# Token sums on VectorE, and the output products of experts 0 to 5 inside the routed loop's last six steps

## The reference

```
gate_logits = x @ gate_weight.T                 # 16 experts
top_vals, top_idx = top_k(gate_logits, 2)
routing_w = softmax(top_vals)
h = silu(einsum('td,efd->tef', x, w1))          # w1[e]: 256 x 512
h_sum = einsum('tef,te->ef', h, mask)           # sum over the tokens that chose e
h_mean = h_sum / maximum(counts, 1)[:, None]
y_mean = einsum('ef,edf->ed', h_mean, w2)       # w2[e]: 512 x 256
out = einsum('tk,tkd->td', routing_w, y_mean[top_idx])
```

## Time and profile before

| | us |
|---|---|
| median of 3 runs | 1165.25 |
| the profiled execution's own time | 1164.0 |
| its span in the trace | 1162.4 |
| start of the first tile's matmuls (L1925) | 1039.07 |
| end of the routed loop's matmuls, start of the last sums (L1912) | 1121.20 |
| first output product (L1856) | 1124.69 |
| transposes of `yT` (L1948) | 1148.06 |

### The profile page before, as it was taken

The page is one execution under the profiler, slowest core; times in us unless marked ns, Lnnn a source line. Parts: engine busy times, 40 slices in busy tenths (PEclk is TensorE's granted clock), DMA queues, the critical chain, the costliest instruction groups (busy, mean ns, idle before and its releaser), DMA issues. The chain is left out here.

```text
span 1162.4 us, 19075 instructions
## 1 busy us (share of the span) xinstructions
PE 1063.3 (91%) x5694; PEld 886.5 (76%) x5694; DVE 964.7 (83%) x1633; ACT 839.8 (72%) x1029; POOL 666.6 (57%) x522
## 2 busy tenths in 40 slices
PE   2993999999999999999999999999859998579985
PEld 2772788888888888888888888888647776579983
DVE  6751699999999999999999999999966887684357
ACT  3212799999999999999999999999724544434442
POOL 3245787877878777877788777874241221133410
PEclk9997999999999999999999999999979999779985
DMA  6736766666666666666666666665020311624455
GB/s 180 261 113 147 156 127 135 134 130 132 134 131 132 135 133 132 133 133 128 130 132 133 135 127 138 127 130 134 1 73 10 116 45 45 211 88 132 149 172 182
DMA packets 129067, 148.77 MB, mean 128 GB/s; under 512 B 72573, under 2 KB 81158, under 8 KB 128893
## 3 DMA queue, kind: packets, MB, share of 16 engines
q0 software_dynamic: 38576, 97.54, 39.1%
q1 hardware_dynamic: 89611, 48.75, 15.9%
q10 hardware_dynamic: 786, 1.30, 0.3%
HBM read 137.00 MB, written 15.66 MB: 131 GB/s over the span
## 5 line engine op out<-in xcount | busy, mean ns | idle before, releaser
L1002 PE MATMUL ps<-W2h,w1l_w3l 128*128 128x512 f32 x1264 | 425.8, 398 | 0.0
L797 POOL DMA_INDIRECT gath<-dst_table,idx_sl x158 | 263.6, 1668 | 53.1 <-issue 47.4
L1002 PEld LDWEIGHTS ps<-W2h,w1l_w3l 128*128 128x128 f32 x1264 | 227.1, 189 | 38.5
L1002 PE MATMUL ps<-W2l,w1l_w3l 128*128 128x512 f32 x632 | 247.8, 392 | 0.0
L810 POOL DMA_INDIRECT gath<-src_table,idx_sl x156 | 187.5, 1202 | 102.3 <-PE ps L997 50.7
L1002 PEld LDWEIGHTS ps<-W2l,w1l_w3l 128*128 128x128 f32 x632 | 118.7, 188 | 27.0
L819 POOL TENSOR_TENSOR msg_lo<-act,msg_hi 128x512 fp32r<-128x512 f32 x77 | 122.9, 1596 | 24.9 <-DVE msg_hi L938 24.9
L888 DVE TENSOR_TENSOR agg<-agg,ps 125x512 f32 x166 | 114.1, 687 | 14.5 <-PE ps L1048 7.6
L844 ACT ACTIVATE act<-ps 128x1024 f32<-128x1024 f32 x79 | 81.2, 1027 | 37.0 <-PE ps L1034 37.0
L900 DVE SCALAR_TENSOR_TENSOR act<-act,ps 128x1024 f32<-128x1024 f32 x79 | 96.0, 1215 | 2.1 <-ACT act L865 2.1
L929 DVE TENSOR_TENSOR w1l_w3l<-act,w1l_w3l 128x1024 fp32r<-128x1024 f32 x79 | 96.3, 1219 | 0.0
(11 more groups left out here) (359 smaller groups left out, 2367.4 us busy)
## 6 DMA issues: line engine op xcount, KB each, us to landing
ea_sl<-ea_scr SPq DMA_DIRECT2D x158, 64.0 KB
w_raw<-in_L_ffn_w_dram SPq DMA_DIRECT2D x13, 512.0 KB, 4.4
w_more<-in_L_ffn_w_dram SPq DMA_DIRECT2D x12, 512.0 KB, 8.7
ea_scr<-in_edge_attr_dram POOLq DMA_DIRECT2D x1, 5000.0 KB
w_late<-in_L_ffn_w_dram SPq DMA_DIRECT2D x7, 512.0 KB, 6.2
w_raw<-in_L_gnn_W_dram SPq DMA_DIRECT2D x3, 1024.0 KB, 8.1
gath<-src_table,idx_sl POOLq DMA_INDIRECT x158
gath<-dst_table,idx_sl POOLq DMA_INDIRECT x158, 5.2
```

What stands on the lines that cost most here:

```text
L797: pool.indirect_dma_start(out=gath[:, k, j, :], out_offset=None, in_=dst_table[:, :], in_offset=bass.IndirectOffsetOnAxis(ap=idx_sl[:, p % ...
L1002: return nc.tensor.matmul(ps_2[:, p % 2, j, :], part[:, p % 2, d, j * P:(j + 1) * P], weights[:, d, :], start=False, stop=last)
```

## The change

1. **Token sums.** The two matmuls per tile on TensorE and the addition of two columns on VectorE go. In their place VectorE runs one `scalar_tensor_tensor` per tile, `acc[expert] += hs * valid`, on 128 partitions x 256, one step behind. The sum over the 128 partitions is left to the mean's matmul: ones (128x128) times `acc[:, e, :]` gives the sum on all partitions. `spread_hm`, `hsum` and `hm` go, and with them ScalarE's part. The division by the counts moves to the end, as one operation on `yT`.
2. **`acc` lies where `w_raw` was** (16 KB per partition), so GpSimd zeroes it between its fourth and its fifth gather, and all of `w2` is now loaded over `w1T`. SP loads experts 0 to 9 once 24 tiles have been multiplied, and 10 to 15 once 27 have.
3. **Inside the loop.** TensorE's mean of expert e, for e = 0 to 5, stands at the end of step 29 + e, and VectorE's four products of it in step 30 + e. Means 0 to 5 use the two banks of `ps_s`; 6 to 15 use four banks, `ps_n` and `ps_s`.
4. Each product now waits for the last but one (its scratch `junk_y` has two slots of 256).

```diff
+INSIDE, INSIDE_AT = 6, 29
...
-        w2_more = nc.alloc_sbuf_tensor_at("w2_more", [P, E - WS, KC, FFN], F32, offset=T["w1T_at"])
+        w2_all = nc.alloc_sbuf_tensor_at("w2_all", [P, E, KC, FFN], F32, offset=T["w1T_at"])
...
+        acc = T["w_raw"][:].rearrange("p a (c f) -> p (a c) f", f=FFN)
...
+        def mean_bank(e):
+            if e < INSIDE:
+                return ps_s[:, e % 2, 0:FFN]
+            return (ps_n, ps_s)[(e - INSIDE) // 2 % 2][:, e % 2, 0:FFN]
+
+        def mean_before(e):
+            return e - 2 if e < INSIDE else max(e - 4, INSIDE - 1)
...
-            for e in range(WS):
-                sp.wait_ge(S["w1T_ps"], (E - EARLY) * FC)
-                sp.wait_ge(S["h_ps"], RT * (e + 1) // (WS + 1))
-                sp.dma_start(w2_raw[:, e], w2_rows[e]).then_inc(w2_in[e], 16)
-
-            sp.wait_ge(S["h_ps"], RT)
-            for e in range(WS, E):
-                sp.dma_start(w2_more[:, e - WS], w2_rows[e]).then_inc(w2_in[e], 16)
+            for first, end, t in ((0, 10, 24), (10, E, 27)):
+                sp.wait_ge(S["h_ps"], t)
+                for e in range(first, end):
+                    sp.dma_start(w2_all[:, e], w2_rows[e]).then_inc(w2_in[e], 16)
...
             for t in range(RT):
+                if t == XG:
+                    pool.wait_ge(S["w1T_ps"], WS * FC)
+                    nc.gpsimd.memset(T["w_raw"][:], 0.0).then_inc(S["acc_zeroed"], 1)
...
-            act.wait_ge(S["hm_ready"], 1)
-            for e in range(E):
-                need(act, S["mean_ps"], e - 1)
-                for f in range(FC):
-                    ins = nc.scalar.activation(spread_hm[:, e % 2, f, :], ident[:], ACT.Copy, scale=hm[:, f, e:e + 1])
-                ins.then_inc(S["spread"], 1)
...
+            def products(e):
+                dve.wait_ge(w2_in[e], 16)
+                dve.wait_ge(S["mean_ps"], e + 1)
+                for q in range(KC):
+                    need(dve, S["y_step"], e * KC + q - 1)
+                    nc.vector.tensor_tensor_reduce(out=junk_y[:, q % 2, :], in0=w2_all[:, e, q, :], in1=mean_bank(e), scale=1.0, scalar=0.0,
+                                                   op0=ALU.mult, op1=ALU.add, accum_out=yT[:, q, e:e + 1]).then_inc(S["y_step"], 1)
...
-                    dve.wait_ge(S["sum_ps"], m + 1)
-                    need(dve, S["summed"], m)
-                    nc.vector.tensor_tensor(cols, cols, ps_s[:, m % 2, 0:FC], ALU.add).then_inc(S["summed"], 1)
...
+                    row = acc[:, bass.ds(e, 1), :].rearrange("p a f -> p (a f)")
+                    dve.wait_ge(S["acc_zeroed"], 1)
+                    dve.wait_ge(S["h_act"], m + 1)
+                    need(dve, S["summed"], m)
+                    nc.vector.scalar_tensor_tensor(out=row, in0=hs[:, m % 2, :], scalar=valid[:, m:m + 1], in1=row, op0=ALU.mult, op1=ALU.add).then_inc(S["summed"], 1)
+                if 0 <= t - INSIDE_AT - 1 < INSIDE:
+                    products(t - INSIDE_AT - 1)
...
+            dve.wait_ge(S["y_step"], E * KC)
+            nc.vector.tensor_tensor(yT[:], yT[:], inv[:].unsqueeze(1).to_broadcast([P, KC, E]), ALU.mult).then_inc(S["y_scaled"], 1)
...
-                    for f in range(FC):
-                        ins = nc.tensor.matmul(ps_s[:, m % 2, f:f + 1], hs[:, m % 2, f * P:(f + 1) * P], valid[:, m:m + 1], start=True, stop=True)
-                    ins.then_inc(S["sum_ps"], 1)
...
+                if 0 <= t - INSIDE_AT < INSIDE:
+                    pe.wait_ge(S["summed"], INSIDE_AT - 1)
+                    mean(t - INSIDE_AT)
```

More of the change, by code:

```diff
@@ L1617, in flat, with experts_done @@
             return ap.rearrange("p a b -> p (a b)")
-        def w2_tile(e):
-            return w2_raw[:, e] if e < WS else w2_more[:, e - WS]
+        def experts_done(t):
+            return -(-(P * (t + 1) - TOP_K * NODES) // (P - 1)) - 1
+        def mean_bank(e):
[4 more added lines that the diff above has]
+            return e - 2 if e < INSIDE else max(e - 4, INSIDE - 1)
         GW_PARTS = (range(0, 4), range(4, GWB), range(GWB, BLOCKS))
@@ L1641, in _ @@
                 sp.dma_start(w1_late[:, e - EARLY - WS, 1], w1_rows[e]).then_inc(w1_in[e - EARLY - WS], 16)
-            for e in range(WS):
-                sp.wait_ge(S["w1T_ps"], (E - EARLY) * FC)
-                sp.wait_ge(S["h_ps"], RT * (e + 1) // (WS + 1))
-                sp.dma_start(w2_raw[:, e], w2_rows[e]).then_inc(w2_in[e], 16)
-            sp.wait_ge(S["h_ps"], RT)
-            for e in range(WS, E):
-                sp.dma_start(w2_more[:, e - WS], w2_rows[e]).then_inc(w2_in[e], 16)
+            for first, end, t in ((0, 10, 24), (10, E, 27)):
+                assert 2 * experts_done(t) >= end
+                sp.wait_ge(S["h_ps"], t)
+                for e in range(first, end):
+                    sp.dma_start(w2_all[:, e], w2_rows[e]).then_inc(w2_in[e], 16)
             for t in range(0, BLOCKS, 2):
@@ L1663, in _ @@
             nc.gpsimd.iota(iota_p[:], [[1, P]], base=0, channel_multiplier=0, allow_small_or_imprecise_dtypes=True).then_inc(S["const"], 1)
-            nc.gpsimd.memset(hsum[:], 0.0).then_inc(S["const"], 1)
             for part in (gw3a, gw3b):
@@ L1711, in _ @@
                     act.wait_ge(S["h_ps"], t + 1)
-                    need(act, S["sum_ps"], t - 1)
+                    need(act, S["summed"], t - 1)
                     nc.scalar.activation(hs[:, t % 2, :], ps_n[:, t % 2, 0:FFN], ACT.Silu).then_inc(S["h_act"], 1)
@@ L1746, in _ @@
             orders = order[:].unsqueeze(1).to_broadcast([NB, BLOCKS, E])
-            dve.wait_ge(S["const"], 5)
+            dve.wait_ge(S["const"], 4)
             def largest(src, n, hot):
@@ L1828, in weights @@
                 nc.vector.tensor_tensor(gw[:], hot1[:], hot2[:], ALU.add).then_inc(S["gw_ready"], 1)
-            for t in range(-1, RT + 3):
-                m, n = t - 3, t + 1
+            def products(e):
[5 more added lines that the diff above has]
+                                                   op0=ALU.mult, op1=ALU.add, accum_out=yT[:, q, e:e + 1]).then_inc(S["y_step"], 1)
+            for t in range(-1, RT + 1):
+                m, n = t - 1, t + 1
                 if t == 2:
                     weights()
-                if m >= 0:
-                    e = dve.value_load(expert_i[0:1, m:m + 1], min_val=0, max_val=E - 1)
-                    cols = hsum[:, :, bass.ds(e, 1)].rearrange("p f a -> p (f a)")
-                    dve.wait_ge(S["sum_ps"], m + 1)
-                    need(dve, S["summed"], m)
-                    nc.vector.tensor_tensor(cols, cols, ps_s[:, m % 2, 0:FC], ALU.add).then_inc(S["summed"], 1)
                 if n < RT:
@@ L1842, in _ @@
                     nc.vector.tensor_tensor(xgTl[:, n % 2, :], ps_t[:, n % 2, :], f32(xgTh[:, n % 2, :]), ALU.subtract).then_inc(S["xgT_lo"], 1)
+                if m >= 0:
+                    e = dve.value_load(expert_i[0:1, m:m + 1], min_val=0, max_val=E - 1)
+                    row = acc[:, bass.ds(e, 1), :].rearrange("p a f -> p (a f)")
[5 more added lines that the diff above has]
+                    products(t - INSIDE_AT - 1)
                 if t in LOWER_AT:
@@ L1846, in _ @@
                     nc.vector.tensor_tensor(gw3_part(part, 64), gw_ps_part(part), f32(gw3_part(part, 0)), ALU.subtract).then_inc(S["gw3_lo"], 1)
[L1848 to L1857, removed]
+            for e in range(INSIDE, E):
+                products(e)
+            dve.wait_ge(S["y_step"], E * KC)
+            nc.vector.tensor_tensor(yT[:], yT[:], inv[:].unsqueeze(1).to_broadcast([P, KC, E]), ALU.mult).then_inc(S["y_scaled"], 1)
             dve.wait_ge(S["y3_hi"], 1)
@@ L1896, in _, with mean @@
             pe.wait_ge(S["tiles_ready"], 1)
-            for t in range(-1, RT + 2):
-                m, n = t - 2, t + 1
+            def mean(e):
+                need(pe, S["y_step"], (mean_before(e) + 1) * KC)
+                nc.tensor.matmul(mean_bank(e), ones[:], acc[:, e, :], start=True, stop=True).then_inc(S["mean_ps"], 1)
+            for t in range(-1, RT):
+                n = t + 1
                 if 0 <= t < RT:
@@ L1928, in _ @@
                     ins.then_inc(S["h_ps"], 1)
+                if 0 <= t - INSIDE_AT < INSIDE:
+                    assert experts_done(INSIDE_AT - 1) >= INSIDE
+                    pe.wait_ge(S["summed"], INSIDE_AT - 1)
+                    mean(t - INSIDE_AT)
                 if t in GATES_AT:
@@ L1937, in _ @@
                     ins.then_inc(S["gw_ps"], 1)
[L1939 to L1946, removed]
+            pe.wait_ge(S["summed"], RT)
+            for e in range(INSIDE, E):
+                mean(e)
+            pe.wait_ge(S["y_scaled"], 1)
             for q in range(KC):
```

15 lines of the change are left out of this document (4 added, 11 removed).

## The result

| | before | after |
|---|---|---|
| median, us | 1165.03 (4 runs) | 1152.96 (4 runs, 1150.98 to 1156.78) |
| ratio, 95% interval | | 0.9889 [0.9868, 0.991] |
| the profiled execution's own time | 1164.0 | 1153.83 |
| first matmul of the first tile | 1039.07 | 1042.36 |
| transposes of `yT` | 1148.06 | 1138.11 |

The kernel is faster by 12.1 us; 17.0 was forecast (1148.2). The clean measure is the stretch between the two marks: it shrank by 13.24 us. The first mark came 3.29 us later in the profile of after, though ahead of it only GpSimd's work is changed (it no longer clears `hsum`, and clears `acc` behind its fourth gather); 2.5 us of that were there when VectorE began to rank the experts (1010.68 against 1008.18). Over the eleven profiles of this study the first mark lies anywhere from 1039.04 to 1045.09. So I compare stretches, not absolute times.

What follows compares the result with a forecast made beforehand. TensorE bounds the loop, VectorE the products behind it. 1102.4 + 10.6 + 4.0 + 13.8 + 0.3 = 1131.1 against 1148.06, 17.0 us less, gave 1148.2 us; range 1144 to 1158.

Steps and rivals of the forecast that it cites:

- a PE wait for `xg`: Sign of being wrong: TensorE's transposes in the loop wait for a gathered tile; no such wait was forecast.
- the mean of expert 6: Behind the loop: it waits for the last sum and is hidden by products of expert 5, so no gap.
- loads beside gathers: Late loop: w2 loads run beside gathers, which have 7.1 us and land in 3.7 to 6.0; counted 0.
- gathers slowed: Rival, late loop: gathers get a fourth of 346 GB/s, seven late, 7.4 us; time 1155.6, chance 0.12.
- Gathers shut out: Rival, late loop: SP queue served first, tile 29's gather waits 18.8 us; time 1170, chance 0.04.
- The step: Routed loop: without token sums a step bound by TensorE takes 1.95 us, 0.37 less for each of 28 tiles.
- the mean of expert 0: On TensorE ahead of step 30's transposes: taken as 0.6 us at full clock.
- The new sum: VectorE's token sum in each loop step: 0.42 us, starting 0.81 behind `xgTl`, within the step's slack.
- The sum stretched beside the gathers: Rival, loop: each gather issue lengthens VectorE's sum about 0.5 us, steps 2.2, 7 us; time 1155, chance 0.12.
- Steps on VectorE: Steps 30 to 33, bound by VectorE's products: 2.65 us each, 10.6 in all; steps 34 and 35 2.0 each.
- The clearing: GpSimd's memset of `acc` between fourth and fifth gather: 3.5 us, hidden with 2 to 3 us to spare.
- Experts 6 to 15: Products on VectorE behind the loop: 10 x 1.38 = 13.8 us, no gap at every second expert; scaling 0.3 more.

Runs made afterwards that it cites:

- The free mean: Changed kernel, but from expert 6 on a mean waits only for products of the expert four before, not expert 5's: 1150.46 us, ratio 0.9864.
- the second profile: The changed kernel run again with nothing edited: 1152.35 us, ratio 0.9883.
- the version with halves: Changed kernel with means waiting for expert e-4, sparser w2 loads, and two products in each of the last twelve steps: 1147.32 us, ratio 0.9831.

## Why the prediction was right in direction and short in size

The mechanism was right: TensorE bound the loop and VectorE the tail, and moving work from the one to the other, and from the tail into the loop, gave time in both. One of the prediction's own signs of being wrong came, a PE wait for `xg`. The stretch shrank by 13.24 us where 17.0 were forecast. The difference of 3.8 us, by the prediction's own steps:

**Mis-sized: the mean of expert 6, forecast 0, measured 1.19.** "The mean of expert 6 waits for the last sum and is hidden by the products of expert 5" was a misreading of the code. `mean_before(6)` is max(2, 5) = 5, so it waits for all products of expert 5 and lies between them and those of expert 6. The free mean took it away. It was in the diff, ahead of any run.

**Mis-sized: loads beside gathers, forecast 0, measured 2.1 (2.8 in the second profile).** I compared a gather's cover of 7.1 us with landings of 3.7 to 6.0 us that were measured without 16 loads beside them, and took from the earlier trace rows that the queues go turn by turn. They didn't here: in 1096 to 1107 q1 had 2329 packets and q0 304, nearly eight to one. What fits all the runs is the bytes in a step: 0.78 MB in 1.95 us would be 400 GB/s, more than the 346 that the same loads reached alone. The rival "gathers slowed" had the right place and the right rate: it gave them a fourth of 346 GB/s, 87, and they moved 1.00 MB in those 11 us, 91 GB/s. It priced that at 7.4, since it had seven gathers late, and TensorE waited for at most three; the others had landed when it came to them. "Gathers shut out" didn't come.

**Not in the forecast: the half clock at the loop's start, 1.07 in this profile.** In 1042 to 1048 the granted clock was 0.50, and tile 3 came 6.01 us behind the first matmul, against 4.94 in the kernel before. Of the eleven profiles tile 3 stands at 4.94 to 5.01 in eight, at 6.01 and 6.13 in two and at 3.64 in one, and the same program had 6.01 and 5.01. So I hold it for chance and not for part of the change; what sets it stays open.

**The step.** Where TensorE alone sets it a step is 1.90 us, not 1.95: a sum off TensorE gives 0.42 instead of 0.37. But more steps are late than I allowed: in every changed kernel the ones behind tiles 10, 12, 20 and 21 take about 2.5, 2.3, 2.15 and 2.03, and the eleven from tile 12 to 23 are 3.4 us shorter than before, 0.31 each. With the mean of expert 0 at 0.43 instead of 0.6 (steps of 2.30 and 1.87 in the version with halves), tile 3 to tile 31 took 56.9 apart from the late gathers; forecast were 57.1. Two errors that cancel: that this term came out right is luck.

**The new sum** took 0.48, not 0.42, and stood mostly 0.85 behind `xgTl` instead of 0.81, inside the slack; it never exceeded 0.49. "The sum stretched beside the gathers" didn't come, for two reasons. Only three of the 35 sums met a gather's issue at all (for 0.37, 0.18 and 0.04 us), and where they met it was the issue that grew, not the sum:

```profile
1063.45 1.20 POOL L1683 DMA_INDIRECT xg<-xl_scr,row_i  x1 [0.98 <-PE f_ps_t L1914]
```

```profile
1063.34 0.48 DVE L1849 SCALAR_TENSOR_TENSOR w_raw<-hs,valid,w_raw 128x256 f32 x1 [0.15 <-issue]
```

The one beside 0.18 us of a sum took 1.01, all others in the loop 0.94 to 0.95. In all ten changed profiles the gather that began 0.10 to 0.13 us behind a sum took 1.18 to 1.21. **Steps on VectorE** took 2.61, 2.37, 2.63 and 2.64 (2.65 forecast), and the last two 3.90 together (4.0): 0.45 us better in sum. **The clearing** took 3.52 (3.5) and kept nobody waiting. **Experts 6 to 15** with the scaling took 14.07 (14.1), without the gap at every second expert.

Sum: 1.19 + 2.11 + 1.07 - 0.23 for the steps - 0.45 for VectorE's steps = 3.7 of 3.8.

## What to carry to other kernels

When a bound engine is relieved, its step shortens and every transfer of a step has less time: divide the bytes in flight by the new step, and compare with the rate that the trace shows at its best, before asking how queues share. Loads can then be spread so that the sum stays under it (here 237 GB/s were free, 286 were not). And read every new wait's argument with its numbers put in at the seam between two phases; the one index that the rule treats differently was worth 1.2 us. Work put beside a bound engine is best cut so that both engines' steps are level: two products in each step were 2.5 us faster than four in every step of a shorter stretch.

## Hardware seen that was not expected

- A wait of 2.92 us of TensorE for a gather was followed by half clock (0.50 in 1113.5 to 1115), and the next tile's pitch was 3.56 us instead of 2.3; the waits for gathers of up to 2.10 us were not.
- A small cast on VectorE was held for the rest of GpSimd's clearing: 2.28 us instead of 0.18.
- A gather's issue on GpSimd that began just behind the new sum on VectorE took 1.20 us instead of 0.95; the sum kept its 0.48.
- Loads of 0.52 MB landed in 8.5 to 17.8 us when queued, where the issue on SyncE's queue took up to 5.08 us; paced one per step, 4.9 to 15.9.
